# Routing of each mixture's first block moved into the stage ahead, second biases added last, low weights spread over the first block

## What is computed

```python
x = x + mamba(layernorm(x));      x = x + mixture0(layernorm(x))
x = x + linear_attention(layernorm(x)); x = x + mixture0(layernorm(x))
x = x + retention(layernorm(x));  x = x + mixture1(layernorm(x))
x = x + softmax_attention(layernorm(x)); x = x + mixture1(layernorm(x))

def mixture(x):                       # 15 experts and a shared one, all 128 wide
    probs = softmax(x @ router_W + router_b)
    cw = the three largest probs of a token, 0 for the other experts
    routed = sum over e of cw[e] * (relu(x @ eW1[e] + eb1[e]) @ eW2[e] + eb2[e])
    return relu(x @ sW1 + sb1) @ sW2 + sb2 + routed
```

## Time and profile before

| | |
|---|---|
| median of 3 runs | 2178.54 us (2176.43 to 2179.1) |
| profiled execution | 2175.81 us |
| its span | 2174.1 us |
| mean granted clock of TensorE | 0.939 |
| busy share of the span | PE 86%, DVE 77%, ACT 55%, POOL 42% |

### The profile page before, as it was taken

One profiled execution on the slowest core, in us unless ns is written; L12 is line 12 of the kernel. 1 busy time (PEld: TensorE's weight loads), 2 busy tenths in 40 slices (PEclk: granted clock), 3 DMA queues, 4 the chain that ended last, 5 costly groups with the idle time before them and its releaser, 6 DMA issues. The chain is left out here.

```text
span 2174.1 us, 31063 instructions
## 1 busy us (share of the span) xinstructions
PE 1862.9 (86%) x9650; PEld 1279.9 (59%) x9650; DVE 1684.7 (77%) x4191; ACT 1200.8 (55%) x2004; POOL 903.4 (42%) x881
## 2 busy tenths in 40 slices
PE   6786699998899967674699978999999999988998
PEld 4564577777677723332577755555555555546777
DVE  6996788866788779998788867766766767738886
ACT  3442266653566634443466644665666666556666
POOL 1110255542455522220455544533533544325555
PEclk8998899999899987976799989999999999999999
DMA  3000344420444310000344400000000000004443
GB/s 101 6 5 5 129 147 147 147 73 1 147 152 157 132 40 1 1 0 0 125 155 160 147 0 1 1 1 1 1 1 1 1 1 1 1 1 166 166 168 126
DMA packets 87704, 142.28 MB, mean 65 GB/s; under 512 B 12369, under 2 KB 24337, under 8 KB 87026
## 3 DMA queue, kind: packets, MB, share of 16 engines
q1 hardware_dynamic: 85232, 139.50, 19.1%
q10 hardware_dynamic: 2306, 0.78, 0.2%
HBM read 136.38 MB, written 3.87 MB: 65 GB/s over the span
## 5 line engine op out<-in xcount | busy, mean ns | idle before, releaser
L2356 ACT ACTIVATE soft_prob<-psum 128x1024 f32<-128x1024 f32 (+3 forms) x384 | 302.6, 813 | 203.6 <-PE psum L2236 202.1
L2448 DVE TENSOR_REDUCE soft_mx<-psum 128x1 f32<-128x512 f32 (+2 forms) x352 | 230.8, 687 | 116.3 <-PE psum L2306 79.4
L2306 PE MATMUL psum<-soft_own,soft_stack 128*128 128x512 f32 (+3 forms) x768 | 249.3, 376 | 24.6 <-DVE soft_mx L2444 10.9
L2236 PE MATMUL psum<-soft_stack,soft_own 128*128 128x512 f32 (+3 forms) x768 | 225.3, 376 | 2.8 <-POOL soft_stack L2213 2.2
L2444 DVE CUSTOM_DVE_ANT_0 psum<-psum,s_soft_sel 128x384 f32<-128x384 f32 (+1 forms) x256 | 157.2, 638 | 64.9 <-PE psum L2306 64.1
L2236 PEld LDWEIGHTS psum<-soft_stack,soft_own 128*128 128x128 f32 x768 | 125.2, 189 | 133.1 <-issue 80.0
L2306 PEld LDWEIGHTS psum<-soft_own,soft_stack 128*128 128x128 f32 x768 | 139.8, 193 | 92.6 <-DVE soft_mx L2448 43.0
L2219 POOL TENSOR_SCALAR_AFFINE_SELECT soft_prob<-soft_prob 128x256 f32<-128x256 f32 x256 | 103.0, 409 | 203.6 <-ACT soft_prob L2356 200.7
L163 POOL TENSOR_TENSOR norm_rstd<-norm_mv,s_const_minus_half 128x4 f32<-128x4 f32 x64 | 65.3, 1020 | 272.8 <-DVE norm_mv L158 272.8
L2253 PE MATMUL psum<-soft_prob,soft_v_pad 128*32 128x512 f32 (+3 forms) x1536 | 163.6, 498 | 3.5 <-ACT soft_prob L2356 2.1
L941 POOL TENSOR_TENSOR ffn0a_low<-ffn0a_full,ffn0a_high 128x512 fp32r<-128x512 f32 x80 | 103.4, 1297 | 95.2 <-ACT ffn0a_high L1093 77.1
(11 more groups left out here) (443 smaller groups left out, 4930.1 us busy)
## 6 DMA issues: line engine op xcount, KB each, us to landing
ffn0a_cwb<-ffn0a_cw_dram SPq DMA_DIRECT2D x120, 256.0 KB, 6.5
ffn0b_cwb<-ffn0b_cw_dram SPq DMA_DIRECT2D x120, 256.0 KB, 6.2
ffn1a_cwb<-ffn1a_cw_dram SPq DMA_DIRECT2D x120, 256.0 KB, 6.5
ffn1b_cwb<-ffn1b_cw_dram SPq DMA_DIRECT2D x120, 256.0 KB, 6.2
s_ffn_w<-in_ffn_w SPq DMA_DIRECT2D x4, 1024.0 KB, 8.1
out_x<-x SPq DMA_DIRECT2D x8, 256.0 KB, 7.4
x<-in_x SPq DMA_DIRECT2D x4, 384.0 KB, 7.4
mamba_coef_dram<-mamba_out_coef SPq DMA_DIRECT2D x8, 96.0 KB, 1.6
```

The source lines that it names most:

```text
L2236: ins = pe.matmul(e_ps[:, n % 2, j, low(n):BLK], own[:, u % 3, 2 * pair + j, kt * P:(kt + 1) * P], stack[:, u % HT, qb * BLK + low(n):(qb ...
L2306: ins = pe.matmul(per_head[:, n, :], stack[:, u % HT, i * P:(i + 1) * P], own[:, u % 3, g, half * BLK:half * BLK + width], start=(n == 0), ...
L2356: nc.scalar.activation(prob[:, done % PROBS, :, low(n):BLK], e_ps[:, n % 2, :, low(n):BLK], ACT.Exp, scale=float(HD) ** -0.5).then_inc(exp ...
L2448: nc.vector.tensor_reduce(mx[:, i, half, heads.start:heads.stop], bank[:, 0:width * len(heads)].rearrange("p (g k) -> p g k", k=width), AX ...
```

## The change

The routing becomes a class `Routing`, of which each stage makes one. Its steps `shift`, `exp`, `probabilities`, `largest`, `combine` and `transpose` are those of before with the names changed; what is new in it stands below. The stage ahead of a mixture (mamba, lin, ret, soft) now does the routing of the mixture's block 0, with a Routing of its own, and stores two things to DRAM: the rows of weights, and the whole transposed array of 96 rows that the second biases need. The mixture stage begins with the broadcasts of that store, and after them loads the 96 rows back into `yt`, from where ScalarE copies them at expert 10. The fetch of layer 1's weights comes behind that. The pads of the mixture's own Routing stay at its start.

Inside the mixture stage, the second biases' matmul of a block moves from ahead of expert 0 to expert 15 of `down`. The low weights come in three pieces (experts 0 to 3, 4 to 7, 8 to 15): VectorE makes the first of both layers at the start, GpSimd the second, the first layer's before the experts and the second layer's after expert 1, VectorE the third after experts 3 and 5. The scale of block 1 stands after expert 1, its moments before the experts. In block 0 the tokens and the routing of block 1 come three experts later than in other blocks (`late`).

Routing, the new class:

```diff
+class Routing:
...
+    def pads(self, dve):
...
+        self.nc.vector.memset(self.prob[:, :, E:E + 8 - TOPK], -1.0)
+        self.nc.vector.memset(self.cw[:, :, E:NE], 1.0)
+        self.nc.vector.memset(self.cw_parts[:, :, :], 0.0).then_inc(self.pads_set, 1)
+        dve.wait_ge(self.pads_set, 1)
...
+    def copy(self, act, q):
+        act.wait_ge(self.cwt_ps_ready, q - self.first + 1)
+        if q > self.first:
+            act.wait_ge(self.stored, self.stored_after(q - 1))
+        self.nc.scalar.copy(self.cwx[EXACT:EXACT + NE, :], self.ps[EXACT:EXACT + NE, :, :]).then_inc(self.cwx_ready, 1)
+        self.nc.scalar.copy(self.cwt[:, q % 2, :], self.ps[0:B2_ROWS, :, :]).then_inc(self.cwt_ready, 1)
...
+    def stored_after(self, q):
+        return self.before + 16 * (q + 2)
...
+    def store(self, sp, q):
+        sp.wait_ge(self.cwx_ready, q - self.first + 1)
+        sp.dma_start(self.dram[q % 2, :, :], self.cwx[EXACT:EXACT + E, :]).then_inc(self.stored, 16)
+    def store_first(self, sp):
...
+        self.store(sp, 0)
+        sp.wait_ge(self.cwt_ready, 1)
+        sp.dma_start(self.first_dram[:, :], self.cwt[:, 0, :].bitcast(F32)).then_inc(self.stored, 16)
```

mamba_output:

```diff
+        OUT_BANKS, AHEAD = 4, 1
...
+            route.pads(dve)
...
                 if q == AHEAD + 1:
                     ahead.scale(dve, 0)
+                if q == AHEAD + 3:
+                    dve.wait_ge(*route_loaded)
+                    route.shift(dve, 0)
+                if q == BLOCKS - 2:
+                    route.probabilities(dve, 0)
+                    route.largest(dve, 0, ahead.pause)
+                    route.combine(dve, 0)
...
+        @block.sync
+        def _(sp):
+            route.store_first(sp)
...
+            route.exp(act, 0)
+            route.copy(act, 0)
...
+                if q == AHEAD + 2:
+                    ahead.transpose(pe, 0)
+                if q == AHEAD + 3:
+                    pe.wait_ge(*route_loaded)
+                    pe.wait_ge(ahead.xt_ready, 1)
+                    route.logits(pe, 0, ahead.xt[:, 0, :])
                 if q == BLOCKS - 1:
-                    ahead.transpose(pe, 0)
...
+                    route.transpose(pe, 0)
```

ffn_stage, SP and GpSimd:

```diff
-            if fetch is not None:
-                for dst, src in fetch[0]:
-                    sp.dma_start(dst, src).then_inc(fetch[1], 16)
...
             def spread(q):
-                sp.wait_ge(cwx_ready, q + 1)
-                if q >= 2:
-                    sp.wait_ge(scaled_ready, E * (q - 1))
...
+                    if q >= 2:
+                        sp.wait_ge(scaled_ready, E * (q - 1))
+                    route.store(sp, q)
+                sp.wait_ge(route.stored, route.stored_after(q))
                 for j in range(E // PIECE):
...
             for q in range(BLOCKS):
                 spread(q)
+                if q == 0:
+                    sp.dma_start(yt[0:B2_ROWS, :], route.first_dram[:, :]).then_inc(first_loaded, 16)
+                if q == 0 and fetch is not None:
+                    for dst, src in fetch[0]:
+                        sp.dma_start(dst, src).then_inc(fetch[1], 16)
...
             split_x(0)
-            if split:
-                low_weights(0, 0)
-                pool.wait_ge(cw_ready, 1)
-                low_weights(0, 1)
             norm.invert(pool, 1)
             if split:
-                low_weights(1, 0)
-                low_weights(1, 1)
+                low_weights(w1_parts, w["w1"], (w1_high, 2), w1_pieces)
...
+                    if split and g == 0 and e == 1:
+                        low_weights(w2_parts, w["w2"], (w2_high, 1), w2_pieces)
+                    if e == (6 if g == 0 else 3) and g + 1 < BLOCKS:
                         split_x(g + 1)
```

ffn_stage, TensorE:

```diff
-                for i, (part, xpart) in enumerate(((0, 0), (1, 0), (0, 1))):
+                order = ((0, 0), (0, 1), (1, 0)) if n == 0 else ((0, 0), (1, 0), (0, 1))
...
+                    if split and g == 0 and e in W_PIECES and part == 1:
+                        pe.wait_ge(w1_pieces[W_PIECES.index(e)], 1)
...
+                if e == 0 and g >= 2:
+                    pe.wait_ge(y_copied, g - 1)
+                if e == E:
+                    pe.wait_ge(*((route.cwt_ready, g) if g else (first_ready, 1)))
                     if split and g == 0:
...
-                    pe.matmul(y_ps[:, g % 2, :], b2_parts[:, :], cwt[:, g % 2, :], start=True, stop=False)
...
+                    pe.matmul(y_ps[:, g % 2, :], b2_parts[:, :], route.cwt[:, g % 2, :], start=False, stop=False)
...
-                pe.matmul(y_ps[:, g % 2, :], w2_parts[0][:, e, :], high[:, slot, :], start=False, stop=False)
+                pe.matmul(y_ps[:, g % 2, :], w2_parts[0][:, e, :], high[:, slot, :], start=(e == 0), stop=False)
...
-            route(0)
...
+                late = 3 * (g == 0)
                 up(n)
-                if n == H_BANKS - 1:
-                    transpose_cw(0)
-                    tokens(1)
-                    route(1)
...
-                if e == 0 and 0 < g and g + 1 < more_blocks:
+                if e == late + (g == 0) and g + 1 < more_blocks:
                     tokens(g + 1)
...
+                if e == 3 + late and g + 1 < BLOCKS:
+                    pe.wait_ge(norm.xt_ready, g + 2)
+                    route.logits(pe, g + 1, norm.xt[:, (g + 1) % 2, :])
...
-                    transpose_cw(g + 1)
+                if e == 8 + late and g + 1 < BLOCKS:
+                    route.transpose(pe, g + 1)
```

ffn_stage, ScalarE and VectorE:

```diff
-                for some in (slice(0, W_PIECES[1]), slice(W_PIECES[1], NE)):
-                    nc.scalar.copy(w1_parts[0][:, some, :], w["w1"][:, some, :]).then_inc(w_high, 1)
-            exp(0)
-            if split:
-                nc.scalar.copy(w2_parts[0][:, :, :], w["w2"][:, :, :]).then_inc(w_high, 1)
+                high_weights(1, 0)
+                high_weights(2, 0)
                 nc.scalar.copy(b2_parts[:, :], w["b2"][:, :]).then_inc(b2_high, 1)
-            copy_cwt(0)
-            copy_x(1)
+                high_weights(1, 1)
...
+                late = 3 * (g == 0)
...
+                if split and n == 2:
+                    high_weights(2, 1)
+                if n == 10:
+                    act.wait_ge(first_loaded, 16)
+                    nc.scalar.copy(route.cwt[:, 0, :], yt[0:B2_ROWS, :]).then_inc(first_ready, 1)
+                if e == 1 + late and g + 1 < more_blocks:
...
-                    exp(g + 1)
+                if e == 4 + late and g + 1 < BLOCKS:
+                    route.exp(act, g + 1)
...
+                if e == 8 + late and g + 1 < BLOCKS:
...
+                        act.wait_ge(down_done, NE * g)
+                    route.copy(act, g + 1)
...
-            largest(0)
-            combine_weights(0)
+            route.pads(dve)
+            norm.statistics(dve, 1)
             if split:
+                low_weights(w1_parts, w["w1"], (w1_high, 1), w1_pieces, 0)
+                low_weights(w2_parts, w["w2"], (w2_high, 1), w2_pieces, 0)
                 dve.wait_ge(b2_high, 1)
...
-            norm.statistics(dve, 1)
-            norm.scale(dve, 1)
-            if split:
-                dve.wait_ge(w_high, 3)
-                low_weights(w1_parts, w["w1"], w1_low_rest)
-                low_weights(w2_parts, w["w2"], w2_low_rest)
...
+                if n == 1:
+                    norm.scale(dve, 1)
...
+                if split and n == 3:
+                    low_weights(w1_parts, w["w1"], (w1_high, 2), w1_pieces, 2)
+                if split and n == 5:
+                    low_weights(w2_parts, w["w2"], (w2_high, 2), w2_pieces, 2)
+                late = 3 * (g == 0)
+                if e == 4 + late and g + 1 < BLOCKS:
+                    route.shift(dve, g + 1)
```

linear_attention_stage (and its call):

```diff
+            route.store_first(sp)
...
+                if not more:
+                    pe.wait_ge(norm.xt_ready, BLOCKS + 1)
+                    route.logits(pe, 0, norm.xt[:, BLOCKS % BPB, :])
...
+            route.transpose(pe, 0)
...
+            route.exp(act, 0)
+            route.copy(act, 0)
...
+            route.pads(dve)
...
+                else:
+                    route.shift(dve, 0)
+                    route.probabilities(dve, 0)
+                    route.largest(dve, 0, norm.pause)
+                    route.combine(dve, 0)
                 add(q + 1)
```

retention_stage:

```diff
+            route.store_first(sp)
...
+                if i == BLOCKS - 1:
+                    pe.wait_ge(*route_loaded)
+                    pe.wait_ge(norm.xt_ready, BLOCKS + 1)
+                    pe.wait_ge(ring_used, products_up_to(PAIRS * BLOCKS - 2))
+                    route.logits(pe, 0, norm.xt[:, BLOCKS % 2, :])
...
                 spread(i)
+            route.transpose(pe, 0)
             project(BLOCKS - 1)
...
+            route.exp(act, 0)
+            route.copy(act, 0)
             scale_z(BLOCKS - 1)
...
+            dve.wait_ge(*route_loaded)
+            route.pads(dve)
+            route.shift(dve, 0)
```

(29 more changed lines are left out.)

323 lines of the change are left out of this document (168 added, 155 removed).

## The result

The changed kernel takes 2163.40 us (median of 4 runs, 2160.88 to 2165.68) against 2177.48 us for the kernel before on the same chip (2174.6 to 2179.1). The ratio is 0.9936, with a 95% interval of 0.9919 to 0.9954. A second measurement of the same kernel, on another chip, gave 2158.70 us against 2179.43, 0.9913 (0.9885 to 0.9942). The forecast was 2157 us, with 2145 to 2170. So the gain is 14 to 21 us where 21.4 was forecast: the direction and the mechanism held, and one term of the sum, block 0, was too small.

A forecast was written before the change was run, and what follows sets the result against it. The prediction took the chain of logits, routing, transposes, store and broadcast at mixture starts as the bound. Net gains of 6.3 (ffn0a), 3.5 (ffn0b), 6.3 (ffn1a) and 5.3 (ffn1b), together 21.4 us, turned 2178.54 into 2157, range 2145 to 2170.

The forecast's parts named there:

- block 0: First weighing to block 1's first weighing: moved work adds 3.7 us (0.5 to 7.1) in three stages, 1.4 in ffn0b.
- The starts: Mixture stage's first instruction to first weighing: 19.5, 13.5, 15.4 and 14.9 us before, about 4.1 after where no store is late.
- its signs: What would show it right: starts 4.1 us in ffn1a and ffn1b, 4.5 to 5 with DMA wait in ffn0a and ffn0b.
- mamba's end: Stage ahead of ffn0a: pads, statistics, scale and routing added on VectorE, so ffn0a starts 5.1 us later.
- The ends of the stages ahead: Routing placed there lengthens mamba by 5.1, lin by 4.2, ret by 1.0 and soft by 1.5 us.
- the price of the scale: VectorE's scale of block 1, moved inside block 0: 1.1 us with GpSimd idle, 3.0 at worst, 2.1 taken.
- the absorption: VectorE waits some 4 us in block 0, so of 5.3 us moved work 3.7 is added; ffn0b 1.4 of 2.1.
- The dearer block 0: Rival: moved work meets GpSimd each time, TensorE stays longer at 1.2 GHz; 8 us a stage, 2169 us, chance 0.13.
- The cheaper block 0: Rival: VectorE's waits swallow the moved work, 0.5 us a stage; 2144 us, chance 0.12.
- The rival whose routing doesn't leave the path: Ends of ret and soft grow by 4.2 us, not 1.0 and 1.5; 5.9 less gain, 2163 us, chance 0.04.
- Late weights: The slower rival: block 1's weights arrive late in every stage; with 7 us a stage 2185 us, chance 0.05.
- The rest: Fetch of layer 1, biases' matmul moved from first to last, copy of reloaded first weights: 0 us each.

The follow-up runs named there:

- own_routing: Changed kernel, but each mixture stage routes its own block 0 again at its start; 2202.61 us, 1.0118 of the kernel before.
- copy_early: Changed kernel with ScalarE's copy of block 1's transposed tokens after expert 3, not expert 4, in block 0; 2170.79 us, 0.9956 of the kernel before.
- lows_first: Changed kernel with the last low weights of both layers made before the first weighing in the three splitting stages; 2169.11 us, 0.9954 of the kernel before.
- ends_b2: Changed kernel, routing steps earlier in mamba's end, shift and exponential earlier in lin's, biases' matmul first from block 1 on; 2160.90 us, 0.9914.
- scale_alone: Changed kernel where GpSimd's first low part in block 0 waits for VectorE's scale of block 1; 2163.72 us, 0.9930 of the kernel before.
- pool_lows: Changed kernel with the last low weights of block 0 made by GpSimd, not VectorE; 2172.62 us, 0.9966 of the kernel before.

## Why the prediction came out as it did

**The starts: right, with a slip for ffn0a.** The forecast's sum had 4.1 us in three stages and 4.4 in ffn0b, its signs 4.5 to 5 with a DMA wait in ffn0a and ffn0b; measured 3.8 to 4.0, with that wait in ffn0b alone. The first weighing of ffn0a was forecast for 250.0 and came at 250.68: mamba's end was 1 us longer than forecast, and the first piece of weights came 3.2 us after its issue, at 250.49, just before VectorE was free. The store of 192 KB, which the earlier trace rows only bounded, landed in 2.1 us, and I had taken 2.0. The view of DMA issues shows it and the load back, behind the broadcasts:

```profile
route_first<-mamba_cwt SPq DMA_DIRECT2D x1, 192.0 KB, 2.1
ffn0a_yt<-route_first SPq DMA_DIRECT2D x1, 192.0 KB, 7.3
```

The estimate of 2.45 us by the Trainium skill's "DMA: Bandwidth & Descriptors" (Anatomy of one DMA), whose rule is for transfers that GpSimd issues, would have been 0.35 too long for this store, which SP issues; the measurement decides. own_routing shows that without the early routing none of this shortening is left.

**The ends of the stages ahead: right in sum, not each.** Forecast 5.1, 4.2, 1.0 and 1.5 us (11.8); measured 6.1, 6.6, 0.6 and 2.8 in one execution and 6.3, 3.7, -0.8 and 0.6 in the other, 12.9 on average. So the sum came near by luck: mamba's end was 1.0 to 1.2 us longer than forecast, ret's 0.4 to 1.8 shorter, and lin's and soft's lay above the forecast in one execution and below it in the other. lin varies most, by 2.9 us (soft by 2.2, ret by 1.4). Views by stretch of the last 16 us of lin, of the changed kernel, its second execution and the kernel before:

```profile
525.30:541.30 16.00, 10.48 (x44) 9.10 (x44) 6.57 (x32) 2.48 (x5) 0.00 (x0) 0.53 0.05 13
```

```profile
521.90:537.90 16.00, 7.87 (x52) 6.54 (x50) 8.94 (x36) 2.49 (x5) 0.00 (x0) 0.80 0.05 13
```

```profile
521.80:537.80 16.00, 9.40 (x69) 7.98 (x68) 8.05 (x17) 2.76 (x5) 1.55 (x2) 1.00 0.00 0
```

TensorE's granted clock is 0.53 there in one execution, 0.80 in the other and 1.00 before. With the routing, TensorE has waits behind VectorE in this stretch; that these make the clock fall was not tried by itself. The length of lin goes with the clock: in the eleven profiled executions with the changed kernel's lin, six have 0.51 to 0.57 in its last 16 us and take 73.5 to 74.0 us, five have 0.79 to 0.86 and take 70.8 to 71.8. Which of the two is cause is not shown; own_routing's lin, without the routing, takes 67.0 us at 0.86. Behind VectorE's last add the stage ends after 3.2 us (537.41 + 0.68 to 541.27) instead of 0.9, which is the 2.3 us that I had carried over from mamba's end.

**Block 0: this is the step that was mis-sized.** "I take 2.1 + 3.2 = 5.3 ... so part is absorbed ... I add 3.7, and 1.4 for ffn0b." Measured were 5.6, 6.7 and 6.6 us in the first execution and 4.8, 5.0 and 6.8 in the second, 5.9 on average, and 0.2 and 0.8 for ffn0b; in sum 18.2 us for 13.4. Two things were wrong in it. First the price of the scale: 4.05 us beside GpSimd, above the 3.01 of the earlier trace rows that I had set as the worst. In that row two of the four instructions took 1.28 and 1.30 us beside GpSimd and two 0.34 without it; in the changed kernel three of the four took 1.3 us. Then the absorption. I had counted on 4 us of VectorE's waits, of which the moved work would fill some. That figure was read from 266.00 to 292.50, which is not block 0; in the three split stages VectorE had waited 2.8 to 2.9 us in block 0, and after the change it waits 2.4 to 5.2: at most half a microsecond was swallowed. In ffn0b it had waited 5.4 us, and block 0 hardly grew; but 1.28 us of these were the wait for the second piece of weights, which I had let stand and which is now 0 and 0.2 us, so part of what looks swallowed is that wait, gone. copy_early shows why such waits can't be filled at will: VectorE and TensorE wait for each other in turn in this block, and a wait removed at one place comes back at the next. lows_first says the same in numbers, about 2.4 us of block 0 for 2.5 us of work.

**The dearer block 0, the rival that came nearest:** it had 8 us a stage and gave a reason, that TensorE stays longer at 1.2 GHz. The growth lies between forecast and rival, but the reason is not the one: the clock in block 0 is about as before. The cheaper block 0 (0.5 us a stage) fits ffn0b alone. The rival whose routing doesn't leave the path had 2163 us, which is the first median, but by number only: it had ret's and soft's ends 4.2 us longer, and they grew by 0.6 and 2.8 or by -0.8 and 0.6.

**Late weights: no.** The first weighing of block 1 has no DMA wait ahead of it in any of the four stages, so the slower rival found no place.

**The rest: two tenths a stage that I had put at 0.** The biases' matmul is the same instruction, but its place is not free: 0.9 us in sum by ends_b2. Of the 2.3 to 2.5 us by which the rest grew, 1.4 are not explained by it. By the lengths in ends_b2 nearly all of it lies in ffn0a and ffn0b; what makes it was not settled.

The error of the sum is then 4.8 us for block 0, 1.1 for the ends, 2.4 for the rest and -1.3 for the starts, 7.0 in all: -21.4 became -14.4 on the average of the two executions. The medians, -14.1 and -20.7, lie around it.

## What to carry to other kernels

A chain of small dependent steps at the start of a stage, with a trip through DRAM in it, is worth moving into the stage ahead even at the cost of some 3 us of that stage's end. Work that is moved into a stretch where two engines feed each other should be priced in full; an idle share of a tenth was no place to put it here. Where VectorE and GpSimd run side by side, price their instructions as a pair: shifting one moved most of the collision to the next instructions in scale_alone, and handing VectorE's work to GpSimd cost both in pool_lows.

## What was not expected of the hardware

Which of VectorE's instructions GpSimd slows is sharper than I had thought. The scale of 4 x 128 elements took 1.11 us alone and 4.05 beside GpSimd, a low part of 512 elements 0.69 and 1.81, low weights of 1,024 elements 1.22 and 2.31, a copy of 64 elements 0.2 and 1.1. Such an instruction waits GpSimd's instruction out: in the traces of the two kernels, scale_alone and pool_lows each low part that took over 0.75 us ended 0.55 us after the end of an instruction of GpSimd (in scale_alone above, 1050.93 after 1050.38). So in these traces one meeting cost no more than what was left of GpSimd's instruction, and it is the number of meetings that adds up: three of the scale's four instructions met one each. The weighing, which reads one of its two tensors from PSUM, took 746 ns on average where it lay wholly beside GpSimd's instructions of 512 elements, and 745 ns where GpSimd did nothing. "GPSIMD Engine Reference" of the Trainium skill (Specifications) has GpSimd share its SBUF interfaces with VectorE's instructions that read two tensors from SBUF or run in a two-port mode. The low parts, the low weights and the weighing agree with that. The scale and the copy read one tensor; whether they run in such a mode no run here shows.
